# Row maxima of an attention layer computed for two heads at once, in two row groups of TensorE, in a chain of four attention layers

## The reference

```
tokens = x.reshape(B, C, N).transpose(0, 2, 1)              # N = 1024
qkv = (tokens @ w_proj + b_proj).reshape(B, N, 8, 3 * 32)
q, k, v = jnp.split(qkv, 3, axis=-1)
attn = jnp.einsum('bihd,bjhd->bijh', q, k) * 32 ** -0.5
attn = jax.nn.softmax(attn, axis=2)
res = jnp.einsum('bijh,bjhd->bihd', attn, v).reshape(B, N, 256)
out = res @ w_out + b_out + tokens
```

## Time and profile before

| | us |
|---|---|
| median of 3 runs | 2838.7 (2837.37 to 2839.07) |
| the profiled execution | 2838.16 |
| its span, first to last instruction | 2836.4 |
| PE busy in it | 2652.5 |
| DVE busy in it | 1983.4 |
| ACT busy in it | 1286.8 |
| POOL busy in it | 698.3 |

### The profile page before, as it was taken

One profiled execution on the slowest core, in us unless ns is written; L12 is line 12 of the kernel. 1 busy time (PEld: TensorE's weight loads), 2 busy tenths in 40 slices (PEclk: granted clock), 3 DMA queues, 4 the chain that ended last, 5 costly groups with the idle time before them and its releaser, 6 DMA issues.

```text
span 2836.4 us, 44487 instructions
## 1 busy us (share of the span) xinstructions
PE 2652.5 (94%) x15932; PEld 1852.8 (65%) x15932; DVE 1983.4 (70%) x2297; ACT 1286.8 (45%) x1874; POOL 698.3 (25%) x444
## 2 busy tenths in 40 slices
PE   5899999999999999999999999999999999999994
PEld 4457775577656776567755777557775577656772
DVE  2665777666976768766786677766787666876666
ACT  2463435533365434644346343563435534364334
POOL 0440025300372014600236002540035300361011
PEclk7899999999999999999999999999999999999997
DMA  5300023000410005000050002300032000500016
GB/s 127 71 1 16 12 65 77 17 1 12 105 38 17 1 12 112 31 17 1 30 124 2 17 12 51 91 12 5 12 73 69 17 1 12 112 31 1 1 62 275
DMA packets 46238, 123.51 MB, mean 44 GB/s; under 512 B 9905, under 2 KB 21425, under 8 KB 42417
## 3 DMA queue, kind: packets, MB, share of 16 engines
q1 hardware_dynamic: 46000, 120.36, 15.9%
HBM read 41.96 MB, written 23.86 MB: 23 GB/s over the span
## 4 chain that ended last, share of the span: by engine, by line
PE 71%; issue 9%; DVE 6%; ACT 4%; SPq 4%; POOL 3%; DMA 2%; DVEq 0%; ACTq 0%; POOLq 0%
PE tile L1542 21%; PE pv L1542 11%; PE pv L1666 8%; PE tile L1628 7%; PE tile L1656 6%; PE tile L1801 4%; PE tile L1692 4%; SPq L582 3%; PE pv L1656 2%; PE tile L1823 2%; PE tile L1852 2%; DMA stack<-qk_r 1%; ACT p L854 1%; POOL qk_r L687 1%; PE tile L1720 1%
## 5 line engine op out<-in xcount | busy, mean ns | idle before, releaser
L1123 DVE TENSOR_REDUCE small<-tile 128x1 f32<-128x1024 f32 x512 | 600.0, 1216 | 130.8 <-PE tile L1628 128.2
L854 ACT ACTIVATE p<-tile 128x512 f32<-128x512 f32 (+1 forms) x632 | 405.2, 692 | 239.2 <-PE tile L1656 214.4
L745 POOL TENSOR_TENSOR row_sum<-act 128x256 f32<-128x256 f32 x32 | 41.6, 1318 | 1475.8 <-DVE act L1316 1475.8
L1542 PE MATMUL tile<-qk_r 128*128 128x512 f32 x1536 | 378.0, 395 | 0.0
L1628 PE MATMUL tile<-stack 96*128 96x512 f32 x1024 | 344.7, 436 | 19.9 <-DMA stack<-qk_r 14.9
L715 POOL TENSOR_TENSOR acc<-acc,p 128x1024 f32<-128x1024 f32 x144 | 339.2, 2385 | 4.1 <-ACT p L854 3.9
L1542 PEld LDWEIGHTS tile<-qk_r 128*128 128x128 f32 x1536 | 287.4, 188 | 66.2 <-issue 7.7
L1321 DVE TENSOR_TENSOR pl<-p,ph 128x1024 fp32r<-128x1024 f32 x128 | 158.2, 1236 | 220.8 <-ACT p L936 220.8
L1628 PEld LDWEIGHTS tile<-stack 96*128 96x128 f32 x1024 | 178.7, 192 | 188.3 <-issue 118.9
L1656 PE MATMUL tile<-stack 112*128 112x512 f32 x760 | 269.6, 420 | 24.9 <-ACT p L854 18.4
L1666 PE MATMUL pv<-p,v 128*32 128x512 f32 x2048 | 273.1, 610 | 1.4 <-ACT p L854 1.4
(11 more groups left out here) (286 smaller groups left out, 4507.2 us busy)
## 6 DMA issues: line engine op xcount, KB each, us to landing
stack<-qk_r SPq DMA_DIRECT2D x192, 256.0 KB, 5.0
x_in<-in_x_dram SPq DMA_DIRECT2D x8, 1024.0 KB, 5.0
act<-in_x_dram SPq DMA_DIRECT2D x8, 1024.0 KB, 4.9
x_scratch<-act SPq DMA_DIRECT2D x7, 1024.0 KB, 4.0
z_scratch<-act SPq DMA_DIRECT2D x7, 1024.0 KB, 3.9
stack<-ones SPq DMA_DIRECT2D x16, 256.0 KB, 4.7
w3f<-w3f_scratch SPq DMA_DIRECT2D x8, 512.0 KB, 3.3
fin_rest<-z_scratch SPq DMA_DIRECT2D x3, 1024.0 KB, 8.5
```

Of the source, the lines that this page charges most:

```text
L854: sc.activation(p0[:, jt % DEPTH, pair, first:first + len(heads) * HALF], tile_wait(batch, "st0", *u, jt, k), ACT.Exp, scale=float(D) ** - ...
L1123: ve.tensor_reduce(maxima[:, h * NT + it:h * NT + it + 1], t, X, ALU.max).then_inc(vector_done, vector.one("max0", g, h, it))
L1542: ins = mm(out, lhs[a][kt_], rhs[c][kt_], start=first and kt_ == 0 and m == 0, stop=last and kt_ == n - 1 and m == 2)
```

## The change

1. `s0` uses only the high parts: 32 rows instead of 96. A call takes two heads: head 2·pair in one row group of 32 partitions, head 2·pair + 1 in the next, both for the same 128 queries and one half of the keys, each into its own half of the tile. Two calls, for the two halves of the keys, take the place of one call per head, so the number of tiles and matmuls stays. `max0` reduces a tile to two columns in `parts0`, and `max_both` takes the larger of the two halves of the keys.
2. For that the high parts of head h must stand in row group h of the stack: `ROWS`, `IMAX_OF`, `K0_OF`. Head 3's maxima then lie at partitions 64 to 95, and its score matmul has 128 rows.
3. In the head of a turn `s0` reads `qk_r` itself and no longer the stack; the wait for the copies moves to `st0` of unit (0,0). The calls there go in twos, and `mt`, `qk0(1, 1)` and the `z` halves move by one.
4. In a key tile the second `s0` moves behind the four `st0`, just before the values; the first stays first.
5. Maxima are turned as they are, without negation and without parts. The sign comes with the spread (`minus8`, or -1.0 in a `scalar_tensor_tensor`), in one fp32r part. VectorE spreads heads 0 and 3, ScalarE heads 1 and 2. The other layers lose the copy `neg_copy`.
6. Three dummies in unit (0,0), jt 0, behind the second `s0`.

```diff
+ROWS = ((0, 1, 2), (1, 0, 2), (2, 0, 1), (3, 0, 1))
+IMAX_OF = (96, 96, 96, 64)
+NMAX_OF = (NMAX, NMAX, NMAX, 2 * NMAX)
+K0_OF = (IMAX + NMAX, IMAX + NMAX, IMAX + NMAX, P)
+TURNED = (0, 0, 0, G * NT - NT)
+VECTOR_ROWS = (0, 3)
+SCALAR_ROWS = slice(1, 3)
...
     if next_unit(g, half):
-        return ("s0", 0), ("st0", 0), ("st0", 1), ("s0", 1), ("st0", 2), ("st0", 3)
+        return ("s0", 0), ("st0", 0), ("st0", 1), ("st0", 2), ("st0", 3), ("s0", 1)
...
                 def s0(g, h, it):
-                    if it == 0 or it == HT:
-                        pe.wait_ge(stacked[g][h], 48 * batch_of(("s0", g, h, it)) + 48)
+                    pair, part = divmod(h, 2)
+                    ahead = of_head(("s0", g, h, it))
+                    if ahead and (h, it) == (0, 0):
+                        scalar_wait("qk0_hi", 1, 0)
+                    elif not ahead and it % HT == 0 and part == 0:
+                        for q in range(2):
+                            pe.wait_ge(stacked[g][2 * pair + q], 48 * batch + 48)
                     o = free("s0", g, h, it)
-                    for s in halves:
-                        ins = mm(o[:, s], stack[0:IMAX, g, 0, h, it * P:(it + 1) * P], stack[0:IMAX, g, 1, h, s],
-                                 start=True, stop=True)
+                    for q in range(2):
+                        rows = slice(D * (2 * pair + q), D * (2 * pair + q) + D)
+                        i = slice(it * P, (it + 1) * P)
+                        queries, keys = ((qk_r[rows, g, t, 0, n] for t, n in ((0, i), (1, halves[part]))) if ahead else
+                                         (stack[rows, g, t, 2 * pair + q, n] for t, n in ((0, i), (1, halves[part]))))
+                        ins = mm(o[:, halves[q]], queries, keys, start=True, stop=True)
...
                 def max0(g, h, it):
                     t = tile_wait("s0", g, h, it)
-                    ve.tensor_reduce(maxima[:, h * NT + it:h * NT + it + 1], t, X, ALU.max
+                    pair, part = divmod(h, 2)
+                    ve.tensor_reduce(parts0[:, 2 * pair:2 * pair + 2, it, part], t.rearrange("p (q n) -> p q n", q=2), X, ALU.max
...
                 def m0(g, half):
-                    vector_wait("neg_lo", g, half)
+                    vector_wait("max_both", g, half)
...
+                            if u == UNITS[0] and jt == 0 and (kind, k) == ("s0", 1):
+                                if body:
+                                    pe.wait_ge(scalar_done, scalar.at(b, "z_kept", 1))
+                                warm(pv[:, HALF:N], 3)
```

More of the change, by code:

```diff
@@ L119, in tensor_steps @@
     s += [("kt", 0), ("qk0", 0, 0), ("qk0", 1, 0), ("kt", 1), ("qv",)]
-    for k in range(G * HT):
-        s += {1: [("mt",)], 2: [("qk0", 0, 1), ("g",)], 4: [("smt", 0), ("smt", 1)], 7: [("qk0", 1, 1)], 11: [("z", 0)]}.get(k, [])
-        s += [("s0", *rows_of(UNITS[0], k))]
+    for k in range(0, G * HT, 2):
+        s += {2: [("mt",), ("qk0", 0, 1), ("g",)], 4: [("smt", 0), ("smt", 1)], 6: [("qk0", 1, 1)], 10: [("z", 0)]}.get(k, [])
+        s += [("s0", *rows_of(UNITS[0], k)), ("s0", *rows_of(UNITS[0], k + 1))]
     s += [("z", 1), ("m0", *UNITS[0])]
@@ L208, in vector_steps @@
         s += [("max0", *rows_of(UNITS[0], k))]
-    s += [(n, *UNITS[0]) for n in ("neg_hi", "neg_copy", "neg_lo")]
-    s += [("max_rows", *UNITS[0], h) for h in range(G // 2)]
+    s += [("max_both", *UNITS[0])]
+    s += [("max_rows", *UNITS[0], h) for h in VECTOR_ROWS]
     for u in UNITS:
@@ L221, in vector_steps @@
         if following:
-            s += [(n, *following) for n in ("neg_hi", "neg_copy", "neg_lo")]
-            s += [("max_rows", *following, h) for h in range(G // 2)]
+            s += [("max_both", *following)]
+            s += [("max_rows", *following, h) for h in VECTOR_ROWS]
     s += [("stat", 1, 0, ct) for ct in range(CT)]
@@ L1160, in max_rows @@
                     ts = slice(half * HT, (half + 1) * HT)
-                    negate((g, half), G, ts, ("max0", *rows_of((g, half), G * HT - 1)))
+                    own("max0", *rows_of((g, half), G * HT - 1))
+                    ve.tensor_reduce(maxima.rearrange("p (h t) -> p h t", h=G)[:, :, ts], parts0[:, :, ts], X, ALU.max
+                                     ).then_inc(vector_done, vector.one("max_both", g, half))
                     t = tile_wait("m0", g, half)
-                    for h in range(G // 2):
-                        spread(stack[IMAX:K0, g, 0, h, half * HALF:(half + 1) * HALF], t[0:NMAX, h * P:(h + 1) * P], ts
+                    for k, h in enumerate(VECTOR_ROWS):
+                        rows = slice(IMAX_OF[h], IMAX_OF[h] + NMAX_OF[h])
+                        spread(stack[rows, g, 0, h, half * HALF:(half + 1) * HALF], t[0:NMAX_OF[h], k * P:(k + 1) * P],
+                               ident[0:NMAX_OF[h], TURNED[h] + ts.start:TURNED[h] + ts.stop], -1.0
                                ).then_inc(vector_done, vector.one("max_rows", g, half, h))
@@ L1949, in turn @@
                     qk0(0, 1, (0,))
-                for k in range(G * HT):
-                    if body and k == 1:
+                for k in range(0, G * HT, 2):
+                    if body and k == 2:
                         mt_tile()
```

96 lines of the change are left out of this document (50 added, 46 removed).

## The result

The changed kernel takes **2949.9 us** (median of 4 runs, 2941.8 to 2958.9) against 2838.7 for the kernel before: a ratio of 1.039, with a 95% interval of 1.036 to 1.043. The prediction said slower as the likeliest (2859 us), but the time lies far outside its range of 2792 to 2880. So some 90 of the 111 us that were lost are not in its sum. The profiled execution is the longest of the four, with 2958.9 us, 120.7 more than that of before.

The account below looks back on a forecast made before the run. PE (TensorE) was taken to bound the key-tile step, with ScalarE close behind. Steps +56, jt 0 and 7 −11, head −14 and turn 0 −10 gave +21 us: 2859 us, against a median of 2838.7 before; range 2792 to 2880.

Parts of the forecast that it names:

- steps jt 1 to 6: Key-tile steps of units with a following one: 3.49 us instead of 3.08, 136 such steps, +56 us in all.
- four in a row: Four score tiles in succession on a ring of three half banks: the fourth waits for ScalarE, costing 0.47 us.
- a visit to another shape: A pair of maxima products beside full-array work: PE pays for the array's change of shape, 0.44 us instead of 0.23.
- jt 7: Last key tile of a unit, priced together with jt 0: 2.29 us instead of 2.56, 40 steps, −11 us in all.
- `qk0(1, 1)` in the head: Start of a turn: this product moves ahead by a tile, 2.0 us earlier in each of seven turns, −14 us.
- turn 0: First turn, no other work in its head: fewer copies come before the first exponential, 89.8 instead of 99.65, −10 us.
- small operations, dummies: Small operations at a unit's end and three dummies at jt 0: covered by PE's other work or waits, priced at nothing.
- rival 4: Granted clock falling after the wait for the copies: sparser work may bring it to every turn, 4 x 1.7, 2866 us; chance 0.03.
- the first: Rival: row groups cost no change of shape beside values and scores, a pair is 0.23 everywhere, 2795 us; chance 0.30.
- the second rival: The two products of a pair run one after the other: 2878 us, or 2935 with changes of shape; chance 0.08.
- the price between: A pair's price between the forecast's 0.44 us and 0.23; at half the extra price 2827 us; chance 0.16.
- The third: Rival: the head doesn't move, since something else holds `qk0(1, 1)`: 2873 us; chance 0.05.

Follow-up runs that it names:

- run 3: The kernel before with only the change's order of a key tile (four score tiles in a row), maxima still on 96 rows: 2902.3 us, ratio 1.023.
- run 4: The kernel before with the new key-tile order and the maxima's products on 32 rows, one head after the other, nothing side by side: 3265.2 us, ratio 1.149.
- run 1: The changed kernel with VectorE's logit operations two maxima later and ScalarE's exponential of them behind the two `smt` copies: 2916.7 us, ratio 1.028.
- run 7: The changed kernel without its own three dummies and without the wait ahead of them: 2983.7 us, ratio 1.053.
- run 8: The changed kernel with the logit operations moved two maxima later and five dummies filling the wait for the copies: 2875.5 us, ratio 1.013.
- run 11: The changed kernel with moved logit operations, five dummies in the wait for the copies, and `minus8` allocated last: 2862.3 us, ratio 1.0081.
- run 5: The changed kernel with five full-array dummies where PE waits 1.25 us for the copies: 2906.1 us, ratio 1.026.
- run 2: The changed kernel with the old order of a key tile, pairs and all else as in the change: 2871.4 us, ratio 1.012.
- run 12: The changed kernel with the old order of a key tile and the logit operations two maxima later: 2852.7 us, ratio 1.007.
- run 6: The changed kernel with one full-array dummy in each step jt 2 to 6 of unit (0,0): 2916.8 us, ratio 1.029.
- run 9: The kernel before with an unused 32-byte tensor placed where the change adds `minus8`, no instruction altered: 2857.6 us, ratio 1.0067.
- run 10: The kernel before with an unused 64-byte tensor placed where the change adds `minus8`: 2843.2 us, ratio 1.0017.

## Why the prediction was wrong

It had the sign, and most of its terms, but not the size. The terms in its own order:

| term | forecast | measured |
|---|---|---|
| steps jt 1 to 6 | +0.41 us each (3.49) | +0.39 (3.47) |
| of it, four in a row | 0.47 | 0.46 (run 3) |
| of it, a visit to another shape | 0.21 | 0.195 (run 4) |
| jt 7 | −0.27 | −0.11 (3.43 against 3.54) |
| `qk0(1, 1)` in the head | −2.0 | −1.95 in the one turn without collision; −2.27 in run 1; +0.75 with it (first turn) |
| turn 0 | −10 | −6.1 |
| small operations, dummies | 0 | the dummies cost 0, but 34 us without them (run 7) |
| addresses | not priced | +1.1 a turn; 13 us between runs 8 and 11 |
| collision with POOL | not priced | 33 us (run 1) |
| slow units | rival 4: 1.7 a turn, 7 in all | 11.3 a unit; 44 us (run 5) |

With collision and slow units repaired and the old addresses the changed kernel takes 2862.3 us, 3 from the forecast of 2859. So **the sum was near for a kernel in which the rest stays as it was, and two things didn't**. That it comes within 3 us is in part luck: the filled wait also takes away the three clock falls of the kernel before, 4.5 us together, which the sum left in, and the smaller misses of the table partly cancel.

*The step that failed first* is the fourth rival: "sparser work may bring it to every turn, 4 x 1.7". The direction was seen and the price taken from the earlier trace rows, a fall that is over within a step. It was given 0.03. What the runs show in its place is 11.3 us for each slow unit (four of them and turn 0 in the profiled execution), 44 us in all. The trace of before can't show it, because its unit has no 32-row products; the prediction should have said that the price of 1.7 rests on how fast the clock comes back, and that this was bounded by no row. With a unit as the far bound (a step at half clock lasts some 2 us longer, times seven, times eight turns) the range would have reached past 2950.

*The second* is the head: "ScalarE, POOL and SP hand it on", −2.0 us a turn, where the six turns that collided take 2.7 to 4.9 more than before and 33 us hang on it (run 1). Moving a product earlier moves POOL's low part earlier as well, and the prediction followed that part down its own chain and didn't ask what lies beside it. In the kernel before, the four logit operations end at 415.34 and POOL starts at 415.71, 0.4 us behind them. The Trainium skill (SBUF — State Buffer, section SBUF: two separate sides) says that a VectorE operation with two SBUF inputs and a GpSimd operation that reads SBUF exclude each other for the whole instruction, and that the one that starts first keeps the ports. The trace agrees: VectorE's operation is in flight for 2.34 us where POOL's record begins 0.023 us or more ahead of it, and for 0.15 at 0.020 or less, where POOL's takes 0.04 us longer instead. Run 1 also shows the other half of the rule: the maximum that reads PSUM runs beside the same POOL instruction undisturbed.

*Turn 0:* the second batch of copies was put at 71.9 and started at 74.81. The first twelve copies started 1.1 us later than assumed and took 14.22 instead of 13.75, the two for the ones took 2.45 instead of 1.2, and the second twelve 15.03 instead of 13.75. The exponential followed them a little sooner than before, and came 3.7 us later than forecast.

*Jt 7 and the unit's end* were 0.16 us less good than forecast at each jt 7, and from the last step of a unit to the first values of the next it is 10.96 us against 10.70 before. This was not taken apart.

*Of the rivals:* the first, the second and the price between are excluded by run 4 and the step. A pair pays 0.2 us for its visit, and its two products do run side by side (0.43 us, where two in a row on 32 rows take 0.66 in run 4). The second price given for the second rival, 2935, doesn't follow from its terms: 45 pairs at 0.21 us in eight turns are 76 us on top of 2878, 2954. Nothing hangs on it. The third, that the head doesn't move, came true in six turns, by a wait that the prediction had not named.

## What to carry to other kernels

A step that moves earlier moves everything that hangs on it, on every engine: for each instruction that arrives at a new time, ask what runs on the other engines at that time, POOL beside VectorE's two-operand operations first. A clock fall is not priced by its length in the old kernel: if the work after it changes to products on few rows, it can last a whole unit, and filling the pause ahead of it with full-array products is a cheap remedy (5 x 0.24 us in each turn saved 44 here). And taking the change apart paid: its head alone, with the filled pause, is faster than either kernel, while its pairs beside scores and values cost what they pay in changes of shape.

## What the runs showed of the hardware that was not expected

- After a fall in the loop the granted clock is back within a step where the maxima's products use 96 rows (run 3), and stays at 0.50 to the end of unit (0,0) where they use 32 and the four scores stand in a row (run 4), with PE busy the whole time. With 32 rows and the old order it stays low for part of the unit (runs 2 and 12). Filling a pause of 1.25 us prevents this fall (run 5). How much full-array work would lift the clock again from inside the unit stays open; in turn 0 of run 6 it rose after one dummy.
- The granted clock fell with PE never idle for more than 0.23 us (run 4, at 584.2).
- A VectorE instruction on two columns took 2.34 us instead of 0.15, where POOL's record begins 0.023 to 0.030 us ahead of it, and 0.15 at 0.005 to 0.020.
- A shift of 32 bytes in the addresses of the operands makes products of 512 columns 0.233 us instead of 0.227 in some stretches, 1.1 us a turn, with no instruction altered (runs 9 and 11). That is 0.3% of the time; 64 bytes cost 0.1 us a turn (run 10).
- A visit to products on 32 rows costs PE 0.2 us (3.93 against 3.54 us for a step with two). Between scores and values it is about half on the way in and half on the way out; between values and scores all of it is on the way out (run 4 against run 3).
